# In the last attention of a four-layer kernel, indirect transfers that gather rows add them to the residual rows in place of VectorE

## The reference

```python
def _L2_ffn_ref(...):                       # each row: a shared expert and one of 8 routed experts
    shared_out = _swiglu(x, shared_gate, shared_up, shared_down)
    ...
    return (shared_out + routed_out).reshape(b, s, h)

def _L3_xattn_ref(queries, keys, values, Wq, Wk, Wv, Wo):   # 16 heads of 16, 77 keys
    scores = jnp.einsum('bhqd,bhkd->bhqk', q, k) / jnp.sqrt(jnp.float32(dh))
    scores = jnp.where(scores == 0, NEG_INF, scores)
    attn = jax.nn.softmax(scores, axis=-1)
    ...

x = x + _L2_ffn_ref(_layernorm(x, axis=-1), ...)
x = x + _L3_xattn_ref(_layernorm(x, axis=-1), ctx_1024, ctx_1024, ...)
x = x + _L3_ffn_ref(_layernorm(x, axis=-1), ...)
```

## Time and profile before

| | |
|---|---|
| median of 3 runs | 1160.98 us (1159.98 to 1161.36) |
| the profiled execution | 1159.67 us, span of its instructions 1157.9 us |
| busy share of the span | PE 79%, DVE 49%, ACT 39%, POOL 33% |
| stage a3, from its first transfer to its last statistics | some 938 to 1131 us of the span |
| mean granted TensorE clock | 0.882 of full speed |

### The profile page before, as it was taken

The page is one execution under the profiler, slowest core; times in us unless marked ns, Lnnn a source line. Parts: engine busy times, 40 slices in busy tenths (PEclk is TensorE's granted clock), DMA queues, the critical chain, the costliest instruction groups (busy, mean ns, idle before and its releaser), DMA issues. The chain is left out here.

```text
span 1157.9 us, 18872 instructions
## 1 busy us (share of the span) xinstructions
PE 918.1 (79%) x5686; PEld 617.3 (53%) x5687; DVE 570.1 (49%) x1290; ACT 450.0 (39%) x879; POOL 383.3 (33%) x725
## 2 busy tenths in 40 slices
PE   6688866886799999926777649997999977877763
PEld 4455544775666666714444415664666655545541
DVE  4778854674432212237998532221111125777774
ACT  4355534652132223205666422221222213555654
POOL 5656642455300000046875302110000022566550
PEclk9899987997599999966899869998999986797895
DMA  5599103011111111128310030001111110000002
GB/s 173 166 371 385 44 1 123 10 47 46 54 43 59 58 61 56 55 75 317 129 33 7 1 109 30 25 18 60 46 45 45 36 48 10 15 15 15 2 1 73
DMA packets 72860, 84.16 MB, mean 73 GB/s; under 512 B 8299, under 2 KB 64595, under 8 KB 72787
## 3 DMA queue, kind: packets, MB, share of 16 engines
q1 hardware_dynamic: 68179, 70.65, 18.2%
q0 software_dynamic: 4608, 12.59, 3.3%
HBM read 45.73 MB, written 37.49 MB: 72 GB/s over the span
## 5 line engine op out<-in xcount | busy, mean ns | idle before, releaser
L1718 PE MATMUL PS<-WE,tmp 128*128 x496 | 184.3, 515 | 0.0
L1334 DVE TENSOR_TENSOR tmp<-PS,tmp 128x352 f32<-128x352 f32 (+1 forms) x78 | 47.4, 608 | 264.7 <-ACT tmp L898 264.7
L573 POOL TENSOR_TENSOR tmp<-tmp,small 128x616 f32<-128x616 f32 x96 | 116.7, 1216 | 103.2 <-DVE small L1025 102.6
L898 ACT ACTIVATE tmp<-PS 128x352 f32<-128x352 f32 (+1 forms) x78 | 41.4, 531 | 217.7 <-PE PS L1718 217.7
L788 ACT ACTIVATE tmp<-PS 128x768 f32<-128x768 f32 x96 | 77.9, 811 | 114.5 <-PE PS L1500 113.1
L1718 PEld LDWEIGHTS PS<-WE,tmp 128*128 128x128 f32 x496 | 90.7, 193 | 59.3 <-issue 34.7
L1498 PE MATMUL PS<-ident,tmp 128*128 128x128 f32 x384 | 67.8, 305 | 45.8 <-POOL rsx L560 25.8
L1738 PE MATMUL PS<-WE,tmp 128*128 (+1 forms) x418 | 101.0, 380 | 2.1 <-DVE tmp L1346 2.1
L538 POOL DMA_INDIRECT WE<-ys,slot_u x32 | 32.7, 1021 | 203.0 <-DMA ys<-tmp 193.4
L1413 PE MATMUL PS<-ident,XN 128*128 128x128 f32 x208 | 40.8, 330 | 69.3 <-ACT XN L724 69.3
L724 ACT ACTIVATE XN<-X,SHIFTS,RSTDS 128x256 f32<-128x256 f32 x104 | 56.4, 592 | 79.8 <-POOL SHIFTS L518 79.8
(11 more groups left out here) (254 smaller groups left out, 1652.9 us busy)
## 6 DMA issues: line engine op xcount, KB each, us to landing
xs_regions<-WE SPq DMA_DIRECT2D x11, 1536.0 KB, 13.5
ys<-tmp SPq DMA_DIRECT2D x62, 128.0 KB, 1.7
WE<-in_L_w SPq DMA_DIRECT2D x16, 352.0 KB
tmp<-xs_regions SPq DMA_DIRECT2D x39, 128.0 KB, 2.0
WE<-in_L_rgT SPq DMA_DIRECT2D x8, 512.0 KB
WE<-in_L_ruT SPq DMA_DIRECT2D x8, 512.0 KB
WE<-in_L_rdT SPq DMA_DIRECT2D x8, 512.0 KB
tmp<-xs SPq DMA_DIRECT2D x23, 128.0 KB, 2.0
```

Source lines behind the costliest of these rows:

```text
L573: pool.tensor_tensor(sc, sc, spread(mx[:, q], SK), ALU.add).then_inc(shifted, 1)
L1334: dve.tensor_tensor(HH[:, q, 0:F], PS[:, 2 * q + 1, 0:F], SL[:, q, 0:F], ALU.mult).then_inc(hh_ready, 1)
L1718: last = pe.matmul(PS[:, 2 * q + k, 0:F], XS[:, q, c], w, start=c == 0, stop=c == G - 1)
```

## The change

In a3 the indirect transfer writes to `X` itself and adds the rows that it fetches to what stands there (`compute_op` add). VectorE no longer adds in a3: it waits for the transfers' semaphore, drains, and goes on to the row statistics. The buffers `YG` of a3 and GpSimd's waits on `gathered_used` go away in a3. The stage a2 is as it was. The places of the transfers and of the wait in the order of slots are the same.

```diff
-        YG = dict(a2=(WE[:, (E - 1) * EW:(E - 1) * EW + 2 * T * D], QTf[:, 0:2 * T * D]),
-                  a3=(WE[:, EW:EW + T * D], WE[:, EW + T * D:EW + 2 * T * D]))
-        YG = {stage: [f.rearrange("p (t k d) -> p t k d", t=T, d=D) for f in pair] for stage, pair in YG.items()}
+        YG = [f.rearrange("p (t k d) -> p t k d", t=T, d=D)
+              for f in (WE[:, (E - 1) * EW:(E - 1) * EW + 2 * T * D], QTf[:, 0:2 * T * D])]
...
-        FED = dict(a2=0, a3=B)
...
                             if gather_slot(b, t, k, K) == s:
-                                after(pool, gathered_used, FED[stage] + b - 1 if b >= 2 else 0)
-                                pool.indirect_dma_start(
-                                    YG[stage][b % 2][:, t, k], None, BUFS[fed][1][:, :],
-                                    bass.IndirectOffsetOnAxis(ap=slot_u[:, k, b * T + t:b * T + t + 1], axis=0)
-                                ).then_inc(gathered[b % 2], 16)
+                                rows_of = bass.IndirectOffsetOnAxis(ap=slot_u[:, k, b * T + t:b * T + t + 1], axis=0)
+                                if stage == "a3":
+                                    pool.indirect_dma_start(X[:, b * T + t], None, BUFS[fed][1][:, :], rows_of,
+                                                            compute_op=ALU.add).then_inc(gathered[b % 2], 16)
+                                    continue
+                                after(pool, gathered_used, b - 1 if b >= 2 else 0)
+                                pool.indirect_dma_start(YG[b % 2][:, t, k], None, BUFS[fed][1][:, :],
+                                                        rows_of).then_inc(gathered[b % 2], 16)
...
                 dve.wait_ge(gathered[b % 2], GATHERED[stage] + 16 * K * T * (b // 2 + 1))
                 dve.drain()
+                if stage == "a3":
+                    return
                 for k in range(K):
                     if k:
                         dve.drain()
                     for t in range(T):
-                        x, y = X[:, b * T + t], YG[stage][b % 2][:, t, k]
-                        if stage == "a2":
-                            last = dve.scalar_tensor_tensor(out=x, in0=y, scalar=gate[:, k, b * T + t:b * T + t + 1], in1=x,
-                                                            op0=ALU.mult, op1=ALU.add)
-                        else:
-                            last = dve.tensor_tensor(x, x, y, ALU.add)
+                        x = X[:, b * T + t]
+                        last = dve.scalar_tensor_tensor(out=x, in0=YG[b % 2][:, t, k],
+                                                        scalar=gate[:, k, b * T + t:b * T + t + 1], in1=x,
+                                                        op0=ALU.mult, op1=ALU.add)
                 last.then_inc(gathered_used, 1)
```

## The result

| | kernel before | changed kernel |
|---|---|---|
| median | 1161.17 us (1159.98 to 1162.38, 4 runs) | 1152.42 us (1149.68 to 1154.11, 4 runs) |
| ratio | | 0.9926 [0.9905, 0.9947] |
| profiled execution, its span | 1159.67, 1157.9 us | 1154.11, 1152.4 us |
| mean granted clock | 0.882 | 0.877 |
| busy: TensorE, VectorE, GpSimd | 918.1, 570.1, 383.3 us | 924.7, 555.9, 390.9 us |

Faster by 8.7 us where 15.1 was forecast.

The account below looks back on a forecast made before the run. One path was taken as the bound: add, statistics, scale, `rsx`, transposes. 11.2 + 6.4 - 2.5 = 15.1 us off the profiled 1159.67 gave 1144.6, or 1145.9 as median; range 1141.0 to 1158.

Parts of the forecast that it names:

- Part 1: VectorE's adds leave a3, so the statistics start earlier: 11.2 us gained, 1.78 for each of batches 4 to 7.
- The full-clock batch: In a3, batches of some 17.5 us instead of 20.8 would show the forecast right.
- Part 3: GpSimd's adding issue takes 0.5 us more, counted behind slot `4b - 9` in batches 3 to 7: 2.5 us lost.
- Part 2: TensorE's clock in a3 stays up because its long waits shrink: 6.4 us gained, bounds 0 and 8.8.
- the sign of being wrong: TensorE's PEclk still at 0.84 would be wrong; 0.95 or more was expected from batch 3 on.
- Part 4: The adding transfer's landing, from the same 2.9 us up to double, is hidden from VectorE: 0.
- Late next: On GpSimd, the bias add (577, now 578), not the statistics, is late next ahead of the scale.
- A: TensorE's clock falls as now and the 0.5 extra issue is hidden: gain 11.2, 1149.8 us; chance 0.18.
- B: GpSimd's issue costs 1 to 2.5 us extra, above 2.0 also behind slot `4b - 11`: 1152 to 1158; chance 0.11.

Follow-up runs that it names:

- first_moved: Changed kernel with only the first transfers of batches 3 to 7 (slot `4b - 11`) issued at the end of slot -1: 1146.29 us, ratio 0.9860.
- second_moved: Changed kernel with only the second transfers of batches 3 to 7 (slot `4b - 9`) issued at the end of slot -1: 1149.40 us, ratio 0.9902.
- after_warm: Changed kernel with four unread matmuls filling TensorE's wait behind the first transfer, ahead of the transposes of slots 6, 10, 14 and on: 1149.52 us, ratio 0.9892.
- before_warm: Kernel before with eight unread matmuls on TensorE ahead of the transposes of slots 3, 7, ... 23, adds kept: 1161.87 us, ratio 0.9995.
- after_tail: Changed kernel with spare unread matmuls on TensorE in slots 29, 32, 33 and 34 of a3: 1150.64 us, ratio 0.9908.
- after_bias: Changed kernel with GpSimd's bias add of batches 0 to 5 moved from slot `4b + 10` to slot `4b + 12`: 1151.43 us, ratio 0.9909.

## Why the prediction was right and wrong

**Part 1 was right, in its mechanism and as far as can be read in its size.** No add on VectorE, statistics 0.14 behind 1045, 578 at 1.26, the scale straight behind it, the wait for `rsx` 1.34 where 1.4 was forecast. The first mark came in at 2.5 where 0.76 + 1.82 gave 2.6. The full-clock batch that I named as a sign, some 17.5, is there: 17.66, in the changed kernel only where no transfer is left. It gains 3.2 on the batch before, and the forecast had 1.78 for the adds and 1.4 for the clock there, in a batch that has no transfer.

**Part 3 is the step that failed, by its place.** The size was right, 0.58 more by the medians where I took 0.5. I counted it behind slot `4b - 9` and wrote of slot `4b - 11` that "GpSimd idles for 2.02, which covers it". That idle stands behind `LB` and `rsx` of the slot, ahead of 573, and it ends with VectorE's maximum. It is slack for 573, and none for `rsx`, which stands ahead of it and which TensorE takes as soon as it is there. The row to read was not GpSimd's idle time behind the transfer but TensorE's behind the `rsx` of that slot: in the kernel before it is 0, 0.84 and 0, and where it is 0, `rsx` is there only 0.05 and 0.14 ahead (at 1015.37 and 1056.11, for transposes at 1015.42 and 1056.25), so there was next to no slack. `first_moved` and `second_moved` show the place: without the five issues of slot `4b - 11` the gain is 0.0140, with them 0.0074, and the waits of 1.4 with the slow batches behind them stay where these issues stay. In the place that I did count, 5 x 0.5, the whole issue costs little in the changed kernel as long as the bias add is there: full-clock batches with a transfer in slot `4b - 9` take 17.72 (`first_moved`), those without one 17.66.

**Part 2 failed with it.** I expected the clock to stay up since the waits behind the bias add became 1.4. They did, and it does stay up behind most of them, at 1075.97 here and at 1035.31 and 1053.04 in `first_moved`, but not at 1016.92. In the changed kernel it fell behind the new waits of 1.20 to 1.42, in three batches. By `after_warm` that costs 2.1 each, where I had 0.7 and twice 1.4, from a slope between two batches of the kernel before. In that kernel itself the price stays open, between 0.75 and 1.4 (`before_warm`). The three batches forecast at 7.3 us together brought 2.3. PEclk at 0.83 in the middle of the stage is the sign of being wrong that the prediction had named.

**The end of the stage was left out.** "Batches past the last add, 1100 to the end, are untouched" was true of the instructions and not of the clock. Both kernels wait 1.61 there, at 1109.73 and now at 1099.11; the one stays at 1.00 and the other falls to 0.67, and 5.1 us go. `after_tail` shows that the clock took most of them, 4 us by the profiles. What made the same wait cost the clock in one kernel and not in the other stays open.

**Part 4 was right**: the time from issue to first use grew from 2.9 to 3.95 us (issued at 948.18, statistics at 952.13), 0.6 of it the issue itself, and it is hidden. **Late next**: 578 is last ahead of the scale, as I said, and it bounds the batch where no transfer is in the way, by 0.76 (`after_bias`). Beside a transfer in slot `4b - 9` the other path, from VectorE's maximum through the issue, is as long, which I hadn't seen.

Of the rivals, A and B each hold a part: the clock fell, though behind another wait, and the issue showed in slot `4b - 11`, though it costs far less than the 2 us that I asked for. That the time lies in the range is partly luck: its upper end was set by B, a much dearer issue, which didn't come; what filled the room was a clock that fell in two stretches where I had it up. The sum by the profiles: 15.1, less 4.5 up to mark 6 (10.6 there), less 5.1 behind it, is 5.5.

## What to carry to other kernels

Slack is read for each instruction that stands behind the one that grows, at its own consumer: an engine's idle time further down its queue covers only what stands after it. Where a change shortens some waits of TensorE, look for short new ones elsewhere and price them at both clock levels, also in stretches that the change doesn't touch. A transfer that adds in place needs no buffer, so its issue can be put where nobody waits for that engine; that was worth as much here as all that its dearer issue cost. And an experiment that takes one thing off a path and shows nothing hasn't cleared it while a second path is as long; nor does a filler price the clock before its own length is checked against the wait that it fills.
